# State space stage: one product and one scan per state index over both channel halves

## The reference

```
xn = layernorm(x) ; x_in, z = split(xn @ W_in)
xc = silu(conv(x_in) + conv_b)                 # 4 taps along the tokens
dt_r, Bm, Cm = split(xc @ W_xproj)             # 8 + 16 + 16 columns
dt = softplus(dt_r @ W_dt + b_dt)
for each token:                                # h has 256 channels x 16 indices
    h = h * exp(dt * A) + dt * B * u           # u is xc
    y = sum over the 16 indices of h * C
out = x + ((y + xc * D) * silu(z)) @ W_out
```

## Time and profile before

| what | value |
|---|---|
| time, median of 3 runs | 1926.7 us (1926.41 to 1928.65) |
| span of the profiled execution | 1948.6 us, mean granted TensorE clock 0.916 |
| first product of the stage, last gate | 707.7 us, 1288.0 us |
| VectorE in the whole span | 1491.3 us busy, 77% |
| TensorE in the whole span | 1562.9 us busy, 80% |
| GpSimd in the whole span | 920.7 us busy, 47% |
| ScalarE in the whole span | 953.5 us busy, 49% |

### The profile page before, as it was taken

How to read it: one execution, slowest core, us unless ns; L and a number is a source line. 1 busy time by engine, 2 the same in 40 slices (tenths; PEclk the granted TensorE clock), 3 DMA queues, 4 the chain that set the end, 5 groups by cost and what they waited for, 6 DMA issues and landing times. The chain is left out here.

```text
span 1948.6 us, 31799 instructions
## 1 busy us (share of the span) xinstructions
PE 1562.9 (80%) x10219; PEld 1017.4 (52%) x10219; DVE 1491.3 (77%) x2947; ACT 953.5 (49%) x1491; POOL 920.7 (47%) x938
## 2 busy tenths in 40 slices
PE   8889888989699978977878878769998811699991
PEld 4545547988476632322333333236776611588891
DVE  6899986887488779999989999967777678533335
ACT  3545543575544567657656666436566410011114
POOL 4455442444200147677676677654344100366653
PEclk8999998999899989999988999979999855799996
DMA  4000000000000000000000000020000040466654
GB/s 144 2 0 0 0 1 27 2 2 1 12 1 0 1 1 1 1 1 0 0 1 0 0 0 1 1 78 11 5 9 5 3 145 0 159 209 206 212 171 135
DMA packets 49075, 75.34 MB, mean 39 GB/s; under 512 B 8861, under 2 KB 34821, under 8 KB 48437
## 3 DMA queue, kind: packets, MB, share of 16 engines
q1 hardware_dynamic: 43541, 64.12, 10.5%
q0 software_dynamic: 4544, 9.32, 1.6%
q10 hardware_dynamic: 864, 0.33, 0.1%
HBM read 62.26 MB, written 11.48 MB: 38 GB/s over the span
## 5 line engine op out<-in xcount | busy, mean ns | idle before, releaser
L1506 POOL TENSOR_TENSOR m_hC<-m_h,m_Cs 128x512 f32<-128x512 f32 x256 | 328.2, 1287 | 169.2 <-DVE m_h L1680 122.6
L1788 PE MATMUL PS<-m_hC,identf 128*128 128x512 f32 x512 | 296.5, 662 | 100.9 <-POOL m_hC L1506 99.9
L1680 DVE TENSOR_TENSOR_SCAN m_h<-m_dA,PS 128x512 f32<-128x512 f32 x256 | 312.4, 1220 | 11.2
L1788 PEld LDWEIGHTS PS<-m_hC,identf 128*128 128x128 f32 x512 | 93.0, 203 | 236.4 <-POOL m_hC L1506 208.9
L1675 DVE TENSOR_TENSOR PS<-PS,m_DU 128x512 f32<-128x512 f32 x256 | 178.4, 697 | 19.9 <-issue 3.8
L1616 ACT ACTIVATE m_dA<-m_DT,m_A 128x508 f32<-128x508 f32 x256 | 174.3, 714 | 31.3 <-DVE m_DT L1664 31.1
L1996 ACT ACTIVATE e_Sg<-PS 128x512 f32<-128x512 f32 x71 | 42.4, 597 | 223.0 <-PE PS L2238 178.8
L2238 PE MATMUL PS<-e_xT,e_WT 128*128 128x128 f32 x1136 | 143.8, 281 | 4.9 <-DVE e_xT L2146 3.4
L1608 ACT COPY m_Cs<-PS 128x512 f32<-128x512 f32 x128 | 73.7, 576 | 143.7 <-PE PS L1766 143.5
L2238 PEld LDWEIGHTS PS<-e_xT,e_WT 128*128 128x128 f32 x1136 | 135.4, 195 | 9.3 <-DVE e_xT L2146 7.1
L1935 POOL DMA_INDIRECT e_XG<-token_rows,e_ids x71 | 68.8, 969 | 138.9 <-DVE e_ids L2140 117.6
(11 more groups left out here) (411 smaller groups left out, 3801.6 us busy)
## 6 DMA issues: line engine op xcount, KB each, us to landing
e_WT<-in_w_wgu SPq DMA_DIRECT2D x71, 512.0 KB
token_rows<-X SPq DMA_DIRECT2D x2, 2048.0 KB
e_Y<-expert_rows SPq DMA_DIRECT2D x16, 256.0 KB, 4.0
k_BD<-in_w_bcr SPq DMA_DIRECT2D x1, 2464.0 KB, 9.5
e_w_wd<-in_w_wd SPq DMA_DIRECT2D x1, 2048.0 KB, 7.9
out_dram<-X SPq DMA_DIRECT2D x8, 256.0 KB, 2.4
X<-in_x SPq DMA_DIRECT2D x1, 1792.0 KB, 8.7
x_Cs<-in_ctx SPq DMA_DIRECT2D x8, 154.0 KB
```

What stands on the lines that cost most here:

```text
L1506: nc.gpsimd.tensor_tensor(hC[:, i % ND, :], hst[:, i % ND, :], Cs[:, n % ND, :], ALU.mult).then_inc(s["hC"], 1)
L1680: nc.vector.tensor_tensor_scan(hst[:, i % ND, :], dA[:, i % NA].rearrange("p b l -> p (b l)"), bank(4), 0.0, ALU.mult, ALU.add).then_inc(s ...
L1788: nc.tensor.matmul(bank(5 + ch), c.identf[:, :], hC[:, i % ND, :], start=False, stop=(n == NS - 1)).then_inc(s["yacc"], 1)
```

## The change

Product and scan of a state index run once, over both halves. The product now reads one spread B row, in bank 4, twice (broadcast over the halves) and writes 1024 columns into banks 1 and 2; the scan runs through 1024 columns. The states lie in ND = 2 pairs of buffers instead of 4 single ones, and the C rows keep their four buffers under a name of their own (`NC`). Step numbers stay: VectorE issues the product at the step of ch 0 and the scan at the step of ch 1, and the stages of `SLOT` stand after them as before, so that a stage with an even slot now lies between a product and its scan. `gate` moves from slot 1 to slot 2. Every wait is restated in whole indices; the spread B row has one bank and waits for the product of the index before; PE issues `spread_b` at ch 0 and `spread_c` at ch 1, both two indices ahead.

```diff
-    ND, NA = 4, 8
+    ND, NA, NC = 2, 8, 4
+    SPREAD_B, INPUTS = 4, slice(1, 3)
...
-    SLOT = {"last_c": 0, "gate": 1, ...
+    SLOT = {"last_c": 0, "gate": 2, ...
...
@@ GpSimd, step
-                n = i // CH
-                pool.wait_ge(s["h"], g * NI + i + 1)
-                pool.wait_ge(s["Cs"], g * NS + n + 1)
-                if not first(g, i, ND):
-                    pool.wait_ge(s["yacc"], g * NI + i - ND + 1)
-                nc.gpsimd.tensor_tensor(hC[:, i % ND, :], hst[:, i % ND, :], Cs[:, n % ND, :], ALU.mult).then_inc(s["hC"], 1)
+                n, ch = i // CH, i % CH
+                if ch == 0:
+                    pool.wait_ge(s["h"], g * NS + n + 1)
+                    pool.wait_ge(s["Cs"], g * NS + n + 1)
+                if not first(g, n, ND):
+                    pool.wait_ge(s["yacc"], g * NI + i - CH * ND + 1)
+                nc.gpsimd.tensor_tensor(hC[:, n % ND, ch, :], hst[:, n % ND, ch, :], Cs[:, n % NC, :], ALU.mult).then_inc(s["hC"], 1)
...
@@ ScalarE, step
-                    act.wait_ge(s["h"], g * NI + i - NA + 1)
+                    act.wait_ge(s["h"], g * NS + (i - NA) // CH + 1)
...
@@ VectorE, step
-                if i < CH:
-                    dve.wait_ge(s["du"], g * CH + i + 1)
                 if ch == 0:
+                    if n == 0:
+                        dve.wait_ge(s["du"], g * CH + CH)
                     dve.wait_ge(s["B"], g * NS + n + 1)
-                if not first(g, i, 1):
-                    dve.wait_ge(s["h"], g * NI + i)
-                nc.vector.tensor_tensor(bank(4), bank(1 + n % 2), DU[:, par, ch, :], ALU.mult).then_inc(s["dBu"], 1)
-                dve.wait_ge(s["dBu"], g * NI + i + 1)
+                    if not first(g, n, 1):
+                        dve.wait_ge(s["h"], g * NS + n)
+                    nc.vector.tensor_tensor(PS[:, INPUTS, :], bank(SPREAD_B).rearrange("p (o t) -> p o t", o=1).to_broadcast([P, CH, T]), DU[:, par], ALU.mult).then_inc(s["dBu"], 1)
+                    return
+                dve.wait_ge(s["dBu"], g * NS + n + 1)
                 dve.wait_ge(s["dA"], g * NI + i + 1)
-                if not first(g, i, ND):
-                    dve.wait_ge(s["hC"], g * NI + i - ND + 1)
-                nc.vector.tensor_tensor_scan(hst[:, i % ND, :], ...
+                if not first(g, n, ND):
+                    dve.wait_ge(s["hC"], g * NI + CH * (n - ND + 1))
+                k = (i - 1) % NA
+                nc.vector.tensor_tensor_scan(hst[:, n % ND].rearrange("p c t -> p (c t)"), ...
...
@@ TensorE, spread_b
-                if not first(g, n, 2):
-                    pe.wait_ge(s["dBu"], g * NI + CH * (n - 1))
-                nc.tensor.matmul(bank(1 + n % 2), ...
+                if not first(g, n, 1):
+                    pe.wait_ge(s["dBu"], g * NS + n)
+                nc.tensor.matmul(bank(SPREAD_B), ...
...
@@ TensorE, step
-                if ch == 0:
-                    if n + 1 < NS:
-                        spread_c(g, par, n + 1)
-                    elif left:
-                        spread_c(g + 1, 1 - par, 0)
-                elif n + 2 < NS:
-                    spread_b(g, par, n + 2)
+                    spread_c(0, 0, 1)
+                spread = spread_b if ch == 0 else spread_c
+                if n + 2 < NS:
+                    spread(g, par, n + 2)
                 elif left:
-                    spread_b(g + 1, 1 - par, n + 2 - NS)
+                    spread(g + 1, 1 - par, n + 2 - NS)
```

More of the change, by code:

```diff
@@ L1426, in state_space @@
     dA = sb("dA", [P, NA, GB, P])
[L1427 to L1429 removed]
+    hst = sb("h", [P, ND, CH, T])
+    Cs = sb("Cs", [P, NC, T])
+    hC = sb("hC", [P, ND, CH, T])
     ln, iln = c.ln, {k: (c.sb("m_i" + k, v.shape, F32, ctx) if k not in ("half", "eps") else v) for k, v in c.ln.items()}
@@ L1432, in state_space @@
     bl = lambda ap: ap.rearrange("p (b l) -> p b l", b=GB)
-    SLOT = {"last_c": 0, "gate": 1, "output0": 1, "silu_z": 3, "output1": 3, "rstd": 6, "stats": 6, "norm": 11, "x0": 8, "x1": 9, "x2": 11, "inner_stats": 11,
+    SLOT = {"last_c": 0, "gate": 2, "output0": 1, "silu_z": 3, "output1": 3, "rstd": 6, "stats": 6, "norm": 11, "x0": 8, "x1": 9, "x2": 11, "inner_stats": 11,
             "inner_rstd": 11, "x3": 13, "dt_b_c": 14, "dt0": 15, "inner_norm": 16, "silus": 18, "rest": 18, "dt1": 18, "parts": 19, "last": 20,
@@ L1605, in c_copy @@
                 act.wait_ge(s["C"], g * NS + n + 1)
-                if not first(g, n, ND):
-                    act.wait_ge(s["hC"], g * NI + CH * (n - ND + 1))
-                nc.scalar.copy(Cs[:, n % ND, :], bank(3)).then_inc(s["Cs"], 1)
+                if not first(g, n, NC):
+                    act.wait_ge(s["hC"], g * NI + CH * (n - NC + 1))
+                nc.scalar.copy(Cs[:, n % NC, :], bank(3)).then_inc(s["Cs"], 1)
             def step(g, par, i, left):
@@ L1756, in spread_b @@
                     pe.wait_ge(s["lo"], g + 1)
-                if not first(g, n, 2):
-                    pe.wait_ge(s["dBu"], g * NI + CH * (n - 1))
-                nc.tensor.matmul(bank(1 + n % 2), W["sel"][:, n:n + 1].to_broadcast([96, P]), hi[:, par, :], start=True, stop=True).then_inc(s["B"], 1)
+                if not first(g, n, 1):
+                    pe.wait_ge(s["dBu"], g * NS + n)
+                nc.tensor.matmul(bank(SPREAD_B), W["sel"][:, n:n + 1].to_broadcast([96, P]), hi[:, par, :], start=True, stop=True).then_inc(s["B"], 1)
             def spread_c(g, par, n):
@@ L1787, in step @@
                 pe.wait_ge(s["hC"], g * NI + i + 1)
-                nc.tensor.matmul(bank(5 + ch), c.identf[:, :], hC[:, i % ND, :], start=False, stop=(n == NS - 1)).then_inc(s["yacc"], 1)
+                nc.tensor.matmul(bank(5 + ch), c.identf[:, :], hC[:, n % ND, ch, :], start=False, stop=(n == NS - 1)).then_inc(s["yacc"], 1)
             def output(half):
```

3 lines of the change are left out of this document (2 added, 1 removed).

## The result

The changed kernel takes 1949.2 us (median of 4 runs, 1936.1 to 1950.1), the kernel before 1926.9 beside it: a ratio of 1.0097, 95% interval 1.0075 to 1.0119. It is 22.3 us slower. Three of the four runs lie between 1948.6 and 1950.1, and of the one at 1936.1, whose granted clock was 0.911 against 0.906 and 0.907, there is no trace. The forecast was 1931: the sign was right and the size five times too small. The forecast's own range, 1923 to 1943, was missed; the wider one up to 1952, which takes in part of the second rival, holds the result.

What follows compares the result with a forecast made beforehand. VectorE bounds the kernel before; after the change, a 73.4 us chain does. Six groups +4.6, clock +4.2, first group +1.5, last -6.3 give +4.0 on 1926.7: 1931 us; own range 1923 to 1943, wider 1908 to 1952.

Steps and rivals of the forecast that it cites:

- second rival: TensorE's clock falls in gate to stats and x0 to x3: about 26 us more, 1957 us; chance 0.12.
- chain round the group: Dependent work from one gate through output1, stats, x0 to x3, rest, dt1, corrected0, inputs1 to the next: 73.4 us.
- four waits that were named: VectorE waits before rest (about 3.5 us a group), softplus0 (2), product 0 (1.4) and stats (1).
- first rival: The chain has slack counted as work, VectorE stays the bound: gain about 55 us, 1872, up to 1915; chance 0.20.
- sum per group: Nine chain links from gate to gate in a plain group, added up to 73.4 us.
- first group: Group with no output before it: 75.9 us against 74.33, 1.5 more, clock not included.
- last: Last group, with nothing to prepare, keeps the gain: 60.0 us against 66.38, 6.3 less.
- links 1, 3, 4 and 9: Gate to stats 9.56 us, scan 4 to x0 2.9, x0 to x3 10.54, product 0 to the gate 4.95.
- A slow TensorE clock, hidden before by the slack, now counts: In x0 to x3, about 0.6 us over the shortest on average; over seven groups 4.2 us.
- - 0.11 (two of the gaps): Saving from two fewer gaps in VectorE's product and scan pair, which falls from 4.05 to 3.61 us.
- Link 5: x3 to rest, where rest already waited for hi: 7.29 us, kept at its measured length.
- link 6: Rest to dt1: rest, scan 9, product 10 and gaps 4.3 us, then a spread and sum 1.45.

Runs made afterwards that it cites:

- e6: Changed kernel with VectorE's rest and last and ScalarE's silus and parts one step later; 1931.3 us, ratio to before 1.0023.
- e10: e6 with parts, output1, inputs0 and inputs1 each one step earlier; 1909.8 us, ratio to before 0.9915.
- e11: e10 with the zero matmuls of e3 added; 1898.7 us, ratio to before 0.9854.
- e3: Changed kernel with four zero matmuls into the running sum ahead of the spread at five steps; 1937.7 us, ratio to before 1.0051.
- e1: Changed kernel with rest moved from slot 18 to 19 and last from 20 to 21; 1938.8 us, ratio to before 1.0057.
- e5: Changed kernel with C spread one index ahead at the even step and B two ahead at the odd step, as before; 1940.4 us.
- e2: Changed kernel with the scan split into two of 512 columns and gate back in slot 1, wide product and one B bank kept; 1945.7 us.
- e7: Changed kernel with the edits of e3, e5 and e6 together; 1954.0 us, ratio to before 1.0137.
- e8: Kernel before with the zero matmuls of e3 at the same five steps; 1922.2 us, ratio to before 0.9967.

## Why the prediction was right, and where it was short

**The bound.** That it goes from VectorE's work to a chain round the group was right: products and scans have the forecast lengths, VectorE is busy 63.2 of 77.25 us, the four waits that were named are there, and shortening links (e6, e10) shortens the group with VectorE's work left as it is or up to 0.9 us more. The first rival, VectorE still the bound, got nothing; a version of it comes true only once the chain is cut (e11). The sum per group was 73.4, and 0.6 for the clock; it is 77.3. Six groups were to take 444.2 + 3.6 us and took 463.9: these 16.1, with 1.2 in the first group and 0.6 in the last, are nearly all of the 18 us between forecast and result. That the result lies within the wider range is owed to the second rival, not to the sum.

**The links,** means of the six groups, measured against the forecast: gate to stats 10.71 (9.56); stats, scan 3, product 4, scan 4 7.30 (7.12); to x0 4.35 (2.9); x0 to x3 11.26 (10.54); x3 to rest 7.29 (7.29); rest to dt1 5.46 (5.75); dt1 to corrected0 10.93 (10.9); to the end of inputs1 14.71 (14.42); to the gate 5.33 (4.95). The differences sum to 3.9, and 3.7 of it lie in links 1, 3, 4 and 9, where sums, Dp and projections run at the lower clock in some or all groups. In the group of e3 that runs at full clock the nine are 9.53, 7.34, 2.62, 10.55, 7.29, 6.03, 10.63, 14.68 and 5.19: 73.86, no link more than 0.3 off the forecast.

**The term that was too small** is "A slow TensorE clock, hidden before by the slack, now counts ... about 0.6 over the shortest on average". By the full-clock group of e3 it is 77.3 - 73.9 = 3.4 us a group (an estimate, from one group), of which the zero matmuls give back 1.9. The 0.6 was taken from how x0 to x3 varied before, and there it holds: that link is 0.7 over its shortest now. It left out links 1, 3 and 9, which TensorE's idle time slows as well. Nor does the clock look hidden before: the groups of before run from 70.80 us at 0.98 to 77.46 at 0.83, 1.9 of it a loop stall. The second rival named the mechanism, and for it "TensorE will wait for product 10 and for inputs1 longer than before"; it was put into links 1 and 4, priced at 10 us in three of seven groups, and given 0.12. It came as a smaller loss in every group, and should have been part of the forecast. Against this, the two loop stalls of 1.9 us that the sum carried over show no more among VectorE's waits.

The Trainium skill's page "TensorE: Matmul & The Clock Gate", section "A second HAM failure mode: psum-queue depth-cycling", which the prediction quotes, tells of short pauses between groups of matmuls, by which the clock goes down and up again. The rows at 948.77 and 963.62 agree with that, though the pauses here are waits of 1.51 and 2.80 us for VectorE and not a cycling through banks.

**Smaller terms.** "- 0.11 (two of the gaps)" for the pair took the gaps of 512-column products; behind a product of 1024 columns the gap is 0.19. That is 0.2 for a pair, up to 0.8 on the chain of a group, and 16 x 0.2 = 3.2 of the 7.0 us that VectorE was to save: by its own path it would need about 67 us a group, not 63.8 (an estimate). The first group was to be 2.1 longer, 0.6 for the clock in it, and is 3.3, at a granted clock of 0.87. The last was to be 6.3 shorter and is 5.7. Against the first rival it was said that six of eight gates waited before; with the last one it is seven.

**What the chain's own sum hid.** Link 5 (7.29) was carried over as "the same instructions in the same order", and it measures 7.29 again; e6 takes it to 6.82 and e10 to 6.0. The larger part of e6 is link 6, where rest stood between product 9 and scan 9: behind the scan it is 3.81 instead of 5.46. Where the decay that scan 9 needs still stands behind ScalarE's SiLU block, with its 2.67 us of waiting inside, link 5 takes 0.5 of that back (7.8 in e1). What was queued behind rest was asked; what was queued behind the SiLU block was not. The C row two ahead entered the sum only as a gain ("ScalarE, which now gets C earlier"); with the order of before six groups are 10.4 us shorter (e5), most of it in links 1 and 4.

**What stays open.** Where the 0.19 us behind the wide product come from (e2 shows only with which instruction they go), what a second bank for B or a first product that waits for one half of DU would give, why one run of the changed kernel took 1936.1 us, and what the kernel before would give with an order of its own.

## What to carry to other kernels

When an engine is made faster, work out the chain of dependent work round one period beside each engine's busy time; once the chain is the longer, a faster engine buys nothing here, and moving single instructions in other engines' queues does (here 18 us by four slots in e6, 21.5 by four in e10). Look in every queue for a block that waits in front of work that others need, and price a longer wait of TensorE with the slow matmuls behind it. Edits to an order don't add by themselves: the later SiLU and rest were worth 18 us with one order of the spreads, and with the other the same slots gave a loss (e7).

## What the runs showed of the hardware

Added work made both kernels faster: 20 zero matmuls in a group took TensorE's busy time from 62.7 down to 60.9 us, as the granted clock rose from 0.89 to 0.98, and the group from 77.25 to 75.0 (e3); they took 11 us off the median of e10 (e11) and 5 off that of the kernel before (e8).

A scan that follows a product of 1024 columns starts 0.19 us after it, whether the scan has 1024 or 512 columns; in two steps of 512 columns the four gaps between instructions sum to 0.22, about 0.05 each.

An activation table load took 1.28 us; the instruction ahead of it ended, and the next one began, 0.01 to 0.02 us from it (977.51, 983.82). The Trainium skill ("ScalarE: Activation LUTs", section "What ACT_TABLE_LOAD costs") gives about 1.28 us for the load and some 1.38 more for a drain at each switch. The load agrees; the rows leave no room for such a drain, neither ahead of the load nor behind it.
